# Adding the experts' rows straight into the output, by halves, and gathering expert 1's rows one stage later

## The chip, the cores and the metric

One core of one Trainium2 chip runs the whole layer as one program. The metric is the device time of an execution in microseconds (us). TensorE is PE in the profile, VectorE DVE, ScalarE ACT, GpSimd POOL, and SyncE SP, which here only issues DMAs.

## The reference: two attentions and a mixture of experts

x is [2, 2048, 256] in float32, so 4096 tokens of 256 numbers. The part that the change touches is the last one:

```python
xn = _layernorm(x, axis=-1)
x = x + _L0_attn_ref(xn, ...) + _L0_ffn_ref(xn, ...)

# in _L0_ffn_ref: attention with biases, then
hidden = resid + (ctx @ o_w + o_b)
xt = layer_norm(hidden, ln2_w, ln2_b).reshape(T, D)
probs = softmax(xt @ router_w)            # T = 4096 tokens, E = 16 experts
m1, m2 = one-hot of each token's first and second expert
loc1 = cumsum(m1) - 1; loc2 = cumsum(m2) - 1 + m1.sum(0)
C = 2 * ceil(T / E)                       # 512 slots an expert
m1 = m1 * (loc1 < C); m2 = m2 * (loc2 < C)
g1, g2 = gates of the kept choices, divided by their sum
xin = rows of xt by expert and slot       # [16, 512, 256]
h = gelu(xin @ fc1_w + fc1_b)             # F = 1024
eout = (h @ fc2_w + fc2_b) * (1.0 - 0.2)
moe_out = for each token, the sum of gate * eout over its kept slots
return resid + moe_out
```

A choice beyond an expert's 512 slots is dropped, and slots that no token takes stay empty. With the reference's own inputs the choices are very uneven. The slots taken are 14, 4, 0, 0, 4, 0, 0, 512, 512, 0, 0, 0, 0, 512, 0, 0 for experts 0 to 15: 1558 of 8192.

## The kernel before, in words

Six stages follow one another, each a block of five instruction streams (one for each engine) that ends in a barrier of all five. Within a stage the order on each engine is written out by hand and the streams meet by semaphores.

- stage_a normalises x and makes the queries, keys and values of both attentions in DRAM; stage_b does both attentions, 16 groups of four heads; stage_c (block from L741) adds projection, residual and second norm, writes the tokens' rows xt to the DRAM tensor xt_scratch, keeps `base` (everything that a token gets beside the experts) in SBUF and computes the router's logits.
- stage_d, the routing stage (block from L975). PE and ACT add the first attention's projection to `base`, and SP stores it, eight pieces of 512 KB, as the first 4096 rows of the DRAM tensor sum_scratch (L1081). DVE finds each token's two experts and slots and turns them round: for each of the 64 groups of 128 slots, `rows_of` holds the token's row to read, `sums_of` the row to add to, `slot_gates` the gate. An empty slot reads row 0 and has a row of its own beyond 4095 to add to; sum_scratch has 512 such spare rows. As soon as `rows_of` is there, POOL issues gather_rows (L729) for experts 0 and 1, four indirect DMAs each, 128 rows of 1 KB in one, into the two buffers of `xin`.
- stage_e, the expert stage (block from L1233). For each of 16 experts PE multiplies the rows (turned, L1404) with fc1 (L1417, eight blocks of 128 features) and the result with fc2 (L1432, four tiles of 128 slots). Every matrix is split in a high and a low part, so each product is three matmuls. The transpositions of expert e+1 stand between the two products of expert e. ACT applies gelu (L1385, L1386), DVE makes the low parts (L1328, L1351, L1336) and takes fc2's result out as `eout`, in two halves of two tiles (L1361), which needs b2, fc2's bias for all experts, scaled once by POOL (L1292). POOL then, for each expert: four gathers for expert e+2 (once PE has turned expert e's rows), four scalings of eout by the slots' gates (L1300), and four indirect DMAs that add the 128 rows of each to sum_scratch in DRAM (L1306, the scatter-adds). Two experts' rows can name the same token, so expert e's scatter-adds wait for those of e-1 to land (`summed`). SP loads the weights of the next expert as soon as DVE has split those of the present one.
- stage_f (block from L1449): SP copies the first 4096 rows of sum_scratch to the output, eight DMAs of 512 KB, DRAM to DRAM, and waits for them.

POOL waits once for both halves of an expert's eout before its scalings:

```python
pool.wait_ge(added, e * 2 + 4)
```

Of the kernel before, what the change touches and what calls it, by code (L numbers as in the profile page):

```python
# [16 lines left out]
ALU = mybir.AluOpType  # L17
ACT = mybir.ActivationFunctionType
AX = mybir.AxisListType
F32 = mybir.dt.float32  # L20
# [5 lines left out]
P = 128  # L26
B, S, D = 2, 2048, 256
T = B * S
# [3 lines left out]
CAP = 2 * (T // E)  # L32
# [16 lines left out]
KEEP = 1.0 - 0.2  # L49
SPARE = CAP  # L50
CELLS = E * CAP // P
# [912 lines left out]
def stage_d(nc, weights, scratch, const, keep, late):  # L964


    fc1_w, fc2_w = weights
    ctx_dram, xt_dram, sum_dram = scratch
    base, logits, numbers = keep
# [5 lines left out]
    with ExitStack() as ctx:  # L975
# [88 lines left out]
        @block.sync  # L1064
        def _(sp):
            def load(c):
                b, cc = c // (NCH // B), c % (NCH // B)
                groups = ctx_dram[(B + b) * HG:(B + b + 1) * HG, :, cc * CH:(cc + 1) * CH]
                sp.dma_start(attT[:, c % PLACES], groups.rearrange("(k g) r t -> (g r) k t", k=KD)).then_inc(att_in[c % PLACES], 16)

            tiles = sum_dram[0:T, :].rearrange("(t p) d -> p t d", p=P)
            for c in range(PLACES):
                load(c)
            sp.dma_start(w1[:, :, :], fc1_w[0].rearrange("(h p) f -> p h f", p=P)).then_inc(w1_in, 16)
            sp.dma_start(w2[:, :, :], fc2_w[0].rearrange("(f p) d -> p f d", p=P)).then_inc(w2_in, 16)
            for c in range(NCH):
                sp.wait_ge(base_ready, 2 * (c + 1))
                if c + PLACES < NCH:
                    load(c + PLACES)
                cut = slice(c * TPC, (c + 1) * TPC)  # L1080
                sp.dma_start(tiles[:, cut], base[:, cut, :]).then_inc(base_stored, 16)  # L1081
            sp.wait_ge(base_stored, 16 * NCH)
# [16 lines left out]
        def _(pool):  # L1099
# [5 lines left out]
            pool.wait_ge(rows_ready, 1)  # L1105
            for e in range(2):
                gather_rows(pool, e, xt_dram, xin, rows_of, rows_in)

# [108 lines left out]
def stage_e(nc, weights, scratch, const, keep):  # L1217
# [6 lines left out]
    fc1_w, fc2_w, fc2_b = weights  # L1224
    xt_dram, sum_dram = scratch
    (w1, w2, w1_parts, xin, rows_of, sums_of, slot_gates), (w1_in, w2_in, w1_high, w1_split, rows_in) = keep
# [6 lines left out]
    with ExitStack() as ctx:  # L1233
# [55 lines left out]
        @block.gpsimd  # L1289
        def _(pool):  # L1290
            pool.wait_ge(b2_in, 16)
            pool.tensor_scalar(b2[:, :, :], b2[:, :, :], KEEP, None, ALU.mult).then_inc(b2_scaled, 1)  # L1292
            for e in range(E):
                i, u = e // 2, e % 2
                if e + 2 < E:
                    pool.wait_ge(turned, KD * (e + 1))
                    gather_rows(pool, e + 2, xt_dram, xin, rows_of, rows_in)
                pool.wait_ge(added, e * 2 + 4)
                for j in range(CAP // P):
                    pool.tensor_scalar(scaled[:, u, j, :], eout[:, u, j, :], slot_gates[:, TPE * e + j:TPE * e + j + 1], None,  # L1300
                                       ALU.mult).then_inc(weighed, 1)
                pool.wait_ge(weighed, (e + 3) * (CAP // P))
                if e > 0:
                    pool.wait_ge(summed[1 - u], TURN * (i + u))  # L1304
                for j in range(CAP // P):
                    pool.indirect_dma_start(out=sum_dram, out_offset=bass.IndirectOffsetOnAxis(ap=sums_of[:, TPE * e + j:TPE * e + j + 1], axis=0),  # L1306
                                            in_=scaled[:, u, j, :], in_offset=None, compute_op=ALU.add).then_inc(summed[u], 16)
            for u in range(2):
                pool.wait_ge(summed[u], TURN * (E // 2))
# [135 lines left out]

def stage_f(nc, out, sum_dram):

    PIECES = 8
    with ExitStack() as ctx:  # L1449
        stored = ctx.enter_context(nc.semaphore("f_stored"))  # L1450
        block = ctx.enter_context(nc.Block())
        dst = out.rearrange("b s d -> (b s d)").rearrange("(n p w) -> n p w", n=PIECES, p=P)
        src = sum_dram[0:T, :].rearrange("t d -> (t d)").rearrange("(n p w) -> n p w", n=PIECES, p=P)

        @block.sync
        def _(sp):
            for n in range(PIECES):
                sp.dma_start(dst[n], src[n]).then_inc(stored, 16)
            sp.wait_ge(stored, 16 * PIECES)


def load_constants(nc, w, const, b1_rows):
# [81 lines left out]
def layer(nc, x, w, out):  # L1544
# [6 lines left out]
    xt_dram = nc.dram_tensor("xt_scratch", [T, D], F32).ap()  # L1551
    sum_dram = nc.dram_tensor("sum_scratch", [T + SPARE, D], F32).ap()
    with ExitStack() as ctx:
# [18 lines left out]
        with ExitStack() as late:  # L1572
# [11 lines left out]
            with nc.sbuf_tensor("base", [P, NTILE, D], F32) as base, nc.sbuf_tensor("logits", [P, NTILE, E], F32) as logits, \  # L1584
                    nc.sbuf_tensor("numbers", [P, NUMBERS_SIZE], F32) as numbers:
                stage_c(nc, x, (xn_dram, ctx_dram, xt_dram, rec_dram), const, ((base, logits, numbers), last))
                stage_d(nc, (w["fc1_w"], w["fc2_w"]), (ctx_dram, xt_dram, sum_dram), const, (base, logits, numbers), keep)
            stage_e(nc, (w["fc1_w"], w["fc2_w"], w["fc2_b"]), (xt_dram, sum_dram), const, keep)
        stage_f(nc, out, sum_dram)


# [23 lines left out]
```

## Time and profile before

| | us |
|---|---|
| median of 3 runs | 2424.3 (2418.44 to 2435.3) |
| the profiled execution | 2424.48 |
| its span, first to last instruction | 2422.8 |
| mean granted TensorE clock | 0.947 of full speed |

By stage, from the timeline: the routing stage runs from 1913.2 to 2007.8 us, the expert stage to 2405.7, the copy to the end. Times of the trace count from the span's start. Busy time of an indirect DMA on POOL is the time in which POOL writes its descriptors; the rows move later.

### The profile page before, as it was taken

The numbers are of one execution on the slowest core, as the hardware profiler recorded it, in microseconds if no ns is written. First come the engines' busy times: TensorE is split into PE (matmuls) and PEld (weight loads), VectorE is DVE, ScalarE is ACT, GpSimd is POOL, SyncE is SP. The second block draws the span as 40 slices with busy tenths as digits, with TensorE's granted clock in tenths as the row PEclk, the third lists the DMA queues.
The fourth block names the chain that finished last, engine by engine and source line by source line (L and its number), as shares of the span: only waits on it lengthen the run. The fifth ranks groups of instructions, "written<-read, shape, count | busy, mean of one in ns | idle before, by whom it ended". The sixth has DMA issues, their size and how long they took to land. (4 is left out here: it accounts for less than half of the span.)

```text
span 2422.8 us, 45249 instructions
## 1 busy us (share of the span) xinstructions
PE 2236.6 (92%) x15977; PEld 1286.5 (53%) x15977; DVE 1901.1 (78%) x5771; ACT 1514.4 (63%) x3190; POOL 507.1 (21%) x405
## 2 busy tenths in 40 slices
PE   5995999999999999999999999999996778999994
PEld 2553444444444444444444444444435667999993
DVE  3553999989899899899899899989917886666661
ACT  2541378778788787787787778878871113545441
POOL 0001000110210201101101001001005115778773
PEclk9997699999999899999899999989997798999997
DMA  5997325345154253451632534516018435666563
GB/s 153 294 264 220 36 28 64 43 57 63 20 73 55 37 64 41 59 63 23 78 44 39 71 38 56 63 21 81 3 19 237 155 86 136 145 137 128 133 130 87
DMA packets 145315, 214.54 MB, mean 89 GB/s; under 512 B 54560, under 2 KB 108000, under 8 KB 136672
## 3 DMA queue, kind: packets, MB, share of 16 engines
q1 hardware_dynamic: 132832, 195.27, 40.8%
q0 software_dynamic: 12288, 16.79, 5.6%
q8 instruction: 108, 1.77, 0.3%
q14 instruction: 87, 0.71, 0.1%
HBM read 138.43 MB, written 76.02 MB: 89 GB/s over the span
## 5 line engine op out<-in xcount | busy, mean ns | idle before, releaser
L653 ACT ACTIVATE probs<-s_banks 128x512 f32<-128x512 f32 (+3 forms) x2560 | 1183.5, 539 | 321.9 <-PE s_banks L604 193.1
L690 DVE TENSOR_REDUCE rowmax<-m_banks 128x1 f32<-128x512 f32 x1536 | 966.5, 683 | 64.8 <-PE m_banks L615 59.2
L615 PE MATMUL m_banks<-ks,qs 48*128 48x512 f32 (+3 forms) x2560 | 827.6, 436 | 28.8 <-PEq L89 20.5
L604 PE MATMUL s_banks<-qs,ks 50*128 50x512 f32 (+3 forms) x2560 | 820.3, 429 | 14.7 <-ACT probs L653 7.7
L633 PE MATMUL v_bank<-probs,vs 128*32 128x512 f32 (+3 forms) x5120 | 616.7, 554 | 0.0
L604 PEld LDWEIGHTS s_banks<-qs,ks 50*128 50x128 f32 x2560 | 402.7, 188 | 394.9 <-ACT probs L653 358.5
L615 PEld LDWEIGHTS m_banks<-ks,qs 48*128 48x128 f32 x2560 | 415.9, 193 | 262.0 <-DVE rowmax L690 163.2
L687 DVE CUSTOM_DVE_ANT_0 unused<-m_banks,c_maskq 128x128 bf16<-128x128 f32 (+3 forms) x1024 | 466.8, 486 | 58.5 <-issue 51.2
L550 POOL CAST nparts<-negmax 128x16 fp32r<-128x16 f32 x64 | 12.6, 196 | 1185.5 <-DVE negmax L696 1185.5
L1432 PE MATMUL e_banks<-w_parts,hid_parts 128*128 128x256 f32 x1536 | 189.7, 284 | 1.4 <-DVE hid_parts L1351 1.4
L576 PE MATMUL s_banks<-c_identb,c_later_col 64*128 64x64 bf16 x1024 | 189.2, 197 | 0.0
L576 PE MATMUL s_banks<-c_identb,c_later_col_swapped 64*128 64x64 bf16 x1024 | 189.0, 197 | 0.0
L1432 PEld LDWEIGHTS e_banks<-w_parts,hid_parts 128*128 128x128 f32 x1536 | 185.7, 192 | 2.9 <-DVE hid_parts L1351 2.5
L633 PEld LDWEIGHTS v_bank<-probs,vs 128*32 128x32 f32 x5120 | 101.3, 108 | 156.4 <-issue 81.0
L1417 PE MATMUL e_banks<-xinT,w_parts 128*128 128x512 f32 x768 | 178.8, 392 | 1.5 <-DVE xinT L1336 1.5
L1417 PEld LDWEIGHTS e_banks<-xinT,w_parts 128*128 128x128 f32 x768 | 144.3, 189 | 31.3 <-issue 1.9
L1385 ACT ACTIVATE hid_parts<-e_banks,c_b1T 128x512 fp32r<-128x512 f32 x128 | 89.5, 700 | 113.6 <-PE e_banks L1417 102.8
L1351 DVE TENSOR_TENSOR hid_parts<-e_hid,hid_parts 128x512 fp32r<-128x512 f32 x128 | 100.0, 794 | 46.2 <-ACT e_hid L1386 45.9
L1300 POOL TENSOR_SCALAR scaled<-eout,slot_gates 128x256 f32<-128x256 f32 x64 | 99.4, 1564 | 63.9 <-DVE eout L1361 63.9
L1306 POOL DMA_INDIRECT sum_scratch<-scaled,sums_of x64 | 106.6, 1666 | 19.1 <-issue 14.6
L576 PEld LDWEIGHTS s_banks<-c_identb,c_later_col 64*128 64x128 bf16 x1024 | 95.8, 96 | 26.4 <-issue 5.4
L576 PEld LDWEIGHTS s_banks<-c_identb,c_later_col_swapped 64*128 64x128 bf16 x1024 | 95.3, 96 | 24.2 <-issue 13.3
(185 smaller groups left out, 1740.9 us busy)
## 6 DMA issues: line engine op xcount, KB each, us to landing
w<-in_L_ffn_fc_w SPq DMA_DIRECT2D x32, 1024.0 KB, 5.3
qs<-q_scratch SPq DMA_DIRECT2D x96, 256.0 KB, 8.3
ks<-k_scratch SPq DMA_DIRECT2D x96, 256.0 KB, 10.0
q_scratch<-parts SPq DMA_DIRECT2D x64, 256.0 KB, 4.5
k_scratch<-parts SPq DMA_DIRECT2D x64, 256.0 KB, 4.7
v_scratch<-vt SPq DMA_DIRECT2D x16, 512.0 KB, 7.9
v_in<-v_scratch SPq DMA_DIRECT2D x32, 256.0 KB, 10.7
qs<-mrows SPq DMA_DIRECT2D x512, 2.0 KB
```

Source lines behind the costliest of these rows:

```text
L576: ins = pe.matmul(bank[:, j * HALF:(j + 1) * HALF], const[mask][rows, :], const["identb"][rows, rows], start=False, stop=j == 1)
L604: ins = pe.matmul(bank, ks[rows, slot, h // 2, k * P:(k + 1) * P], qs[rows, slot, h // 2, q * CH + first:(q + 1) * CH], start=True, stop=n ...
L615: pe.matmul(room(("M", NM * group + n))[:, 0:width], qs[rows, slot, h // 2, t * P:(t + 1) * P], ks[rows, slot, h // 2, c * CH:c * CH + wid ...
L633: ins = pe.matmul(v_bank[rows, first:CH], vs[:, slot, k, rows], probs[:, (n * GH + h) % PR, 0:CH - first], start=k == 0, stop=k == TPC * ( ...
L653: act.activation(probs[:, n % PR, 0:width], s_banks[:, (NS * group + n) % SRING, 0:width], ACT.Exp, scale=SCALE).then_inc(p_ready, 1)
L687: dve.tensor_tensor_reduce(unused[:, h, 0:width], scores, const["maskq"][:, CH - width:CH], 1.0, NEG, ALU.add, ALU.max, out).then_inc(m_us ...
L690: dve.tensor_reduce(out, scores, AX.X, ALU.max).then_inc(m_used, 1)
L1300: pool.tensor_scalar(scaled[:, u, j, :], eout[:, u, j, :], slot_gates[:, TPE * e + j:TPE * e + j + 1], None, ALU.mult).then_inc(weighed, 1)
L1306: pool.indirect_dma_start(out=sum_dram, out_offset=bass.IndirectOffsetOnAxis(ap=sums_of[:, TPE * e + j:TPE * e + j + 1], axis=0), in_=scal ...
L1351: dve.tensor_tensor(hid_parts[:, LO, f, :], hid[:, f % HRING, :], f32(hid_parts[:, HI, f, :]), ALU.subtract).then_inc(hid_split, 1)
L1417: last = pe.matmul(banks[:, HBANK + f % HRING, :], w1_parts[:, a, h, f * P:(f + 1) * P], xinT[:, b, h, :], start=h == 0 and (a, b) == PASS ...
L1432: last = pe.matmul(banks[:, OBANK + n, j * D:(j + 1) * D], hid_parts[:, a, f, tile * P:(tile + 1) * P], w2_parts[:, b, f, :], start=f == 0 ...
```

## The change

The stages add to the output `out` instead of sum_scratch, from stage_d's stores on; sum_scratch, its spare rows and stage_f are gone. The scatter-adds get a bounds check: an index above 4095 is to be skipped. stage_d gathers only expert 0's rows, and expert 1's are the first thing that POOL issues in stage_e. And POOL takes eout by halves: two scalings and two scatter-adds when the first half is there, two and two for the second; the wait for expert e-1's scatter-adds stands ahead of the first half's.

```diff
-SPARE = CAP
...
-            tiles = sum_dram[0:T, :].rearrange("(t p) d -> p t d", p=P)
+            tiles = out.rearrange("b s d -> (b s) d").rearrange("(t p) d -> p t d", p=P)
...
             pool.wait_ge(rows_ready, 1)
-            for e in range(2):
-                gather_rows(pool, e, xt_dram, xin, rows_of, rows_in)
+            gather_rows(pool, 0, xt_dram, xin, rows_of, rows_in)
...
         @block.gpsimd
         def _(pool):
+            gather_rows(pool, 1, xt_dram, xin, rows_of, rows_in)
             pool.wait_ge(b2_in, 16)
...
-                pool.wait_ge(added, e * 2 + 4)
-                for j in range(CAP // P):
-                    pool.tensor_scalar(scaled[:, u, j, :], eout[:, u, j, :], slot_gates[:, TPE * e + j:TPE * e + j + 1], None,
-                                       ALU.mult).then_inc(weighed, 1)
-                pool.wait_ge(weighed, (e + 3) * (CAP // P))
-                if e > 0:
-                    pool.wait_ge(summed[1 - u], TURN * (i + u))
-                for j in range(CAP // P):
-                    pool.indirect_dma_start(out=sum_dram, out_offset=bass.IndirectOffsetOnAxis(ap=sums_of[:, TPE * e + j:TPE * e + j + 1], axis=0),
-                                            in_=scaled[:, u, j, :], in_offset=None, compute_op=ALU.add).then_inc(summed[u], 16)
+                for half in range(2):
+                    pool.wait_ge(added, e * 2 + 2 + half + 1)
+                    pair = range(half * TPE // 2, (half + 1) * TPE // 2)
+                    for j in pair:
+                        pool.tensor_scalar(scaled[:, u, j, :], eout[:, u, j, :], slot_gates[:, TPE * e + j:TPE * e + j + 1], None,
+                                           ALU.mult).then_inc(weighed, 1)
+                    pool.wait_ge(weighed, (e + 2) * TPE + pair[-1] + 1)
+                    if e > 0 and half == 0:
+                        pool.wait_ge(summed[1 - u], TURN * (i + u))
+                    for j in pair:
+                        pool.indirect_dma_start(out=rows,
+                                                out_offset=bass.IndirectOffsetOnAxis(ap=sums_of[:, TPE * e + j:TPE * e + j + 1], axis=0),
+                                                in_=scaled[:, u, j, :], in_offset=None, bounds_check=T - 1, oob_is_err=False,
+                                                compute_op=ALU.add).then_inc(summed[u], 16)
...
-def stage_f(nc, out, sum_dram):
...
-            for n in range(PIECES):
-                sp.dma_start(dst[n], src[n]).then_inc(stored, 16)
-            sp.wait_ge(stored, 16 * PIECES)
...
-    sum_dram = nc.dram_tensor("sum_scratch", [T + SPARE, D], F32).ap()
...
-        stage_f(nc, out, sum_dram)
```

On POOL, from the end of the routing stage into expert 0 (the branches L975 and L1289 are the stage's end and the next one's start). Before:

```order
L729 DMA xin<-xt_scratch,rows_of 128x256 [waits rows_ready]
L729 DMA xin<-xt_scratch,rows_of 128x256 x7
L975 UNCONDITIONAL_BRANCH
L1289 UNCONDITIONAL_BRANCH [waits barrier_Pool_Activation_PE_DVE_SP_gather]
L1292 TENSOR_SCALAR b<-b 128x4096 [waits b2_in]
L729 DMA xin<-xt_scratch,rows_of 128x256 [waits e_turned]
L729 DMA xin<-xt_scratch,rows_of 128x256 x3
L1300 TENSOR_SCALAR scaled<-eout,slot_gates 128x256 [waits e_added]
L1300 TENSOR_SCALAR scaled<-eout,slot_gates 128x256 x3
L1306 DMA sum_scratch<-scaled,sums_of 4608x256 [waits weighed]
L1306 DMA sum_scratch<-scaled,sums_of 4608x256 x3
```

The same place with the change:

```order
L728 DMA xin<-xt_scratch,rows_of 128x256 [waits rows_ready]
L728 DMA xin<-xt_scratch,rows_of 128x256 x3
L974 UNCONDITIONAL_BRANCH
L1288 UNCONDITIONAL_BRANCH [waits barrier_Pool_Activation_PE_DVE_SP_gather]
L728 DMA xin<-xt_scratch,rows_of 128x256 x4
L1292 TENSOR_SCALAR b<-b 128x4096 [waits b2_in]
L728 DMA xin<-xt_scratch,rows_of 128x256 [waits e_turned]
L728 DMA xin<-xt_scratch,rows_of 128x256 x3
L1302 TENSOR_SCALAR scaled<-eout,slot_gates 128x256 [waits e_added]
L1302 TENSOR_SCALAR scaled<-eout,slot_gates 128x256
L1308 DMA out<-scaled,sums_of 4096x256 [waits weighed]
L1308 DMA out<-scaled,sums_of 4096x256
```

Four gathers have moved behind the stage's boundary and ahead of the scaling of b2 (the tile b), and the first pair of scalings is followed at once by its pair of scatter-adds. The last expert on POOL, before and with the change:

```order
L1300 TENSOR_SCALAR scaled<-eout,slot_gates 128x256 [waits e_added]
L1300 TENSOR_SCALAR scaled<-eout,slot_gates 128x256 x3
L1306 DMA sum_scratch<-scaled,sums_of 4608x256 [waits summed0,weighed]
L1306 DMA sum_scratch<-scaled,sums_of 4608x256 x3
L1233 UNCONDITIONAL_BRANCH [waits summed1,summed0]
```

```order
L1302 TENSOR_SCALAR scaled<-eout,slot_gates 128x256 [waits e_added]
L1302 TENSOR_SCALAR scaled<-eout,slot_gates 128x256
L1308 DMA out<-scaled,sums_of 4096x256 [waits summed0,weighed]
L1308 DMA out<-scaled,sums_of 4096x256
L1302 TENSOR_SCALAR scaled<-eout,slot_gates 128x256 [waits e_added]
L1302 TENSOR_SCALAR scaled<-eout,slot_gates 128x256
L1308 DMA out<-scaled,sums_of 4096x256 [waits weighed]
L1308 DMA out<-scaled,sums_of 4096x256
L1232 UNCONDITIONAL_BRANCH [waits summed1,summed0]
```

The instructions are the same but for their order; the last two scatter-adds stand behind the second half's two scalings alone.

## Rows read from the trace of the kernel before

**Rows 1.** The page: busy time of the engines; the chain that ended last.

```profile
PE 2236.6 (92%) x15977; PEld 1286.5 (53%) x15977; DVE 1901.1 (78%) x5771; ACT 1514.4 (63%) x3190; POOL 507.1 (21%) x405
...
POOL 11%; issue 4%; PE 1%; DVE 0%; ACT 0%; POOLq 0%; ACTq 0%; DVEq 0%
```

**Rows 2.** Windows: columns, then busy us (instructions) of twelve experts in a row.

```profile
core 0: us, PE busy (x) PEld busy (x) DVE busy (x) ACT busy (x) POOL busy (x), PEclk, DMA share, GB/s
2063.14:2342.50 279.36, 279.36 (x1825) 256.06 (x1824) 187.04 (x240) 136.93 (x222) 215.37 (x144) 1.00 0.63 135
```

**Rows 3.** Timeline of POOL in expert 12 (start us, us, ...); a DVE group.

```profile
2320.06 6.59 POOL L1300 TENSOR_SCALAR scaled<-eout,slot_gates 128x256 f32<-128x256 f32 x4 [2.93 <-DVE eout L1361]
...
2335.99 1.90 POOL L729 DMA_INDIRECT xin<-xt_scratch,rows_of  x1 [0.30 <-issue]
...
L1351 DVE TENSOR_TENSOR hid_parts<-e_hid,hid_parts 128x512 fp32r<-128x512 f32 x96 | 70.3, 742 | 34.1 <-ACT e_hid L1386 33.9
```

**Rows 4.** Timeline: end of the routing stage, start of the expert stage.

```profile
1991.45 1.20 POOL L729 DMA_INDIRECT xin<-xt_scratch,rows_of  x1 [38.05 <-DVE rows_of L1208]
...
2000.49 0.95 POOL L729 DMA_INDIRECT xin<-xt_scratch,rows_of  x1 [0.30 <-issue]
...
2007.87 1.94 PE L1404 MATMUL e_banks<-c_ident,xin 128*128 128x128 f32 x8 [17.21 <-PEq L975]
...
2008.16 0.35 SPq L1277 DMA_DIRECT2D b<-in_L_ffn_fc_b  x1
```

**Rows 5.** Timeline and a window: the last expert and the final copy.

```profile
2388.27 0.69 DVE L1361 SCALAR_TENSOR_TENSOR eout<-e_banks,b 128x512 f32<-128x512 f32 x1 [4.96 <-PE e_banks L1432]
2389.07 3.62 POOL L1300 TENSOR_SCALAR scaled<-eout,slot_gates 128x256 f32<-128x256 f32 x4 [7.89 <-DVE eout L1361]
2392.97 1.59 POOL L1306 DMA_INDIRECT sum_scratch<-scaled,sums_of  x1 [0.28 <-POOL scaled L1300]
...
2398.58 1.55 POOL L1306 DMA_INDIRECT sum_scratch<-scaled,sums_of  x1 [0.31 <-issue]
2405.76 5.46 SPq L1458 DMA_DIRECT2D out<-sum_scratch  x8
...
2402.00:2405.70 3.70, 0.00 (x0) 0.00 (x0) 0.00 (x0) 0.00 (x0) 0.00 (x0) 0.50 0.00 0
```

**Rows 6.** Timeline: the boundary before the routing stage.

```profile
1913.23 1.28 ACT L1087 ACT_TABLE_LOAD   x1 [0.27 <-PEq L741]
```

**Rows 7.** Windows behind the gathers; the last column is GB/s.

```profile
1992.50:2006.60 14.10, 0.00 (x0) 0.00 (x0) 0.16 (x1) 0.00 (x0) 6.80 (x8) 0.55 0.70 74
...
2006.50:2007.00 0.50, 0.00 (x0) 0.00 (x0) 0.00 (x0) 0.00 (x0) 0.00 (x0) 0.50 0.01 0
```

**Rows 8.** Timeline and a window: head of the expert stage.

```profile
2011.30 12.69 PE L1417 MATMUL e_banks<-xinT,w_parts 128*128 128x512 f32 x48 [1.49 <-DVE xinT L1336]
...
2015.31 10.59 POOL L1292 TENSOR_SCALAR b<-b 128x4096 f32<-128x4096 f32 x1 [13.87 <-DMA b<-in_L_ffn_fc_b]
...
2016.92 10.20 DVE L1351 TENSOR_TENSOR hid_parts<-e_hid,hid_parts 128x512 fp32r<-128x512 f32 x5 [2.29 <-ACT e_hid L1386]
...
2023.83 1.03 PE L1404 MATMUL e_banks<-c_ident,xin 128*128 128x128 f32 x8
...
2034.94 0.68 DVE L1361 SCALAR_TENSOR_TENSOR eout<-e_banks,b 128x512 f32<-128x512 f32 x1
...
2039.51 11.07 PE L1417 MATMUL e_banks<-xinT,w_parts 128*128 128x512 f32 x48
...
2009.00:2011.00 2.00, 0.81 (x4) 0.41 (x2) 1.22 (x2) 1.19 (x2) 0.00 (x0) 0.50 0.93 385
```

**Rows 9.** Line L1306: ns lowest, median, highest; the software queue: packets, MB, share.

```profile
L1306 POOL DMA_INDIRECT sum_scratch<-scaled,sums_of x64: 1547/1637/2052, 2047.4 to 2398.6; - x64
...
q0 software_dynamic: 12288, 16.79, 5.6%
```

**Rows 10.** Waits of the DMA queue: us in total, times, longest.

```profile
SPq L1449 <- DMA out<-sum_scratch: 11.2, 1, 11.2
```

More of the change, by code:

```diff
@@ L967, in stage_d @@
     fc1_w, fc2_w = weights
-    ctx_dram, xt_dram, sum_dram = scratch
+    ctx_dram, xt_dram, out = scratch
     base, logits, numbers = keep
@@ L1224, in stage_e @@
     fc1_w, fc2_w, fc2_b = weights
-    xt_dram, sum_dram = scratch
+    xt_dram, out = scratch
+    rows = out.rearrange("b s d -> (b s) d")
     (w1, w2, w1_parts, xin, rows_of, sums_of, slot_gates), (w1_in, w2_in, w1_high, w1_split, rows_in) = keep
@@ L1443, in _ @@
             expert(E // 2 - 1, 1, False)
-def stage_f(nc, out, sum_dram):
[L1448 to L1456, printed above, removed]
-            for n in range(PIECES):
-                sp.dma_start(dst[n], src[n]).then_inc(stored, 16)
-            sp.wait_ge(stored, 16 * PIECES)
 def load_constants(nc, w, const, b1_rows):
@@ L1586, in layer @@
                 stage_c(nc, x, (xn_dram, ctx_dram, xt_dram, rec_dram), const, ((base, logits, numbers), last))
-                stage_d(nc, (w["fc1_w"], w["fc2_w"]), (ctx_dram, xt_dram, sum_dram), const, (base, logits, numbers), keep)
-            stage_e(nc, (w["fc1_w"], w["fc2_w"], w["fc2_b"]), (xt_dram, sum_dram), const, keep)
-        stage_f(nc, out, sum_dram)
+                stage_d(nc, (w["fc1_w"], w["fc2_w"]), (ctx_dram, xt_dram, out), const, (base, logits, numbers), keep)
+            stage_e(nc, (w["fc1_w"], w["fc2_w"], w["fc2_b"]), (xt_dram, out), const, keep)
 _ATTN = ["W_dq", "W_uq", "W_dkv", "W_uk", "W_uv", "W_o"]
```

## The prediction, made before the changed kernel was run

> **What bounds the kernel now.** I read the page first, then the windows of the last stages, then the timelines of the three places that the change touches. Over the whole span PE is busy 92% and POOL 21% [rows 1], and yet the chain that ended last gives POOL the largest share of what it names, 11% [rows 1]. That is a warning about how such a chain is read: through the expert loop it steps from POOL instruction to POOL instruction, but in twelve successive experts PE is busy 279.36 us of 279.36 us [rows 2], 23.28 us each, at the full granted clock (1.00, the 2.4 GHz level), and POOL waits about 2.9 us for DVE's eout before each batch of scalings [rows 3]. So the loop is PE's. What isn't PE's lies at its two ends. Between the last gather of the routing stage and the first transposition of the expert stage no engine computes for 6.4 us [rows 4]. And from the last eout half to the end of the span 33.8 us pass (2388.96 to 2422.8) with PE idle [rows 5], of which the final copy takes 17. The change works on both ends.
>
> **The four gathers of expert 1 leave the routing stage.** POOL issues eight gathers there, one every 1.29 us (starts 1991.45 to 2000.49, seven steps), and has written the last one's descriptors at 2001.44; PE, DVE and SP resume at 2007.87 to 2008.16 [rows 4]. A stage's end alone does not cost that: at the boundary before, where no indirect DMA runs, ACT begins the routing stage's first instruction after 0.27 us of idle time [rows 6]. What fills the 6.4 us is data: the DMA engines carry the gathered rows at 74 GB/s until about 2006.5 [rows 7], some 13.5 us for eight gathers, 1.7 us each, slower than they are issued. So the stage ends 1.4 us behind the last gathered row. With four gathers the data should end 4 x 1.7 = 6.7 us earlier (1999.8), and the issuing, over at 1996.3, stays under it. The other end of the bound is that the boundary follows the issuing: 4 x 1.26 = 5.0 us. I take **-6.7**, since the 6.4 us of silence between issue and resumption are explained by the data and by nothing else that I see.
>
> **They come back at the head of the expert stage.** There POOL waited 13.9 us for the bias b2, which landed 7.1 us after its issue [rows 8], so four gathers of 1.3 to 1.6 us fit ahead of the scaling of b2; expert 1's rows are read by PE at 2023.83, 16 us after the stage's start, and issue (6 us) plus 4 x 1.7 us of data is under that. The price is traffic: 0.5 MB of rows beside b2 and two weight loads. In the profile b2's scaling on POOL (10.6 us) stretches five DVE subtractions to 10.20 us, where five take 3.7 us in the loop (mean 742 ns), and the first expert lasts 28.2 us (2011.30 to 2039.51) in place of 23.3 [rows 2, 3, 8]. If b2 lands later, that stretch moves later by as much. 0.5 MB more at the 385 GB/s of that window is 1.4 us [rows 8]. Bounds: -1 (the stretch falls where DVE is needed less) to +4.9 (the loss that this expert already shows, once more). I take **+1**. Behind the scaling come expert 2's gathers, not read until 2050; expert 0's eout needs the scaled b2 only at 2034.94, 9 us after it is there, so that cover holds a delay up to 9 us. The gathers also move from a stretch where DVE is idle (0.95 us each) to one where it works, where the same instruction took up to 1.90 us [rows 3, 4]; 4 x 1 us more would still be under b2's landing plus its 9 us.
>
> **Scaling and adding by halves.** In the loop POOL's work is 4 scalings (6.6 us, mean 1.6 beside DVE), 4 scatter-adds of 1.64 and 4 gathers, 0.3 us apart [rows 3, 9]; the halves neither add nor remove an instruction there, they start two scalings and two scatter-adds 5.65 us sooner, at the first eout half. Nothing on PE waits for that, so in the loop it is worth **0**: PE covers it. Queued behind POOL's new wait for the second half are the gathers for expert e+2. From the first eout POOL needs 1.8 + 0.3 + 3.5 us for the first half, from 5.7 on 3.3 + 0.3 + 3.5 + 0.3 for the second (to 13.1) and 5.9 for the gathers (to 19.0); the next eout comes at 23.3. POOL's slack is so 4.3 us an expert. At the last expert it counts. Eout's halves are ready at 2383.31 (DVE's idle time before the second starts there) and 2388.96 [rows 5]. Before: four scalings of 0.91 us, then four scatter-adds to 2400.13. After: the first half is done by 2389.0, hidden under PE's second half; behind 2388.96 stand two scalings (1.8), 0.3, and two scatter-adds (1.59 + 0.31 + 1.55), which ends at 2394.6. That is **-5.5**.
>
> **No final copy.** The copy's first DMA is issued at 2405.76; the span ends at 2422.8, with the last wait for its landing lasting 11.2 us to 2422.4 [rows 5, 10]. All of it goes: **-17.0**. What is late next is the landing of the last scatter-add: from the end of its issue to the copy's start 5.6 us pass (1.9 us of data until 2402.0, then 3.7 us of silence) [rows 5]. I keep these 5.6 us as the kernel's new end; the former end had 0.4 us after its last landing, which the 5.6 already hold as a stage's end.
>
> **The bounds check.** No row shows an indirect DMA with one. I bound its price by the nearest row, the scatter-add itself [rows 9]: from -1.6 us each (the indices of empty slots write no descriptors) to a doubling, +1.6 us; I take no change, as all 64 scatter-adds lie between 1.55 and 2.05 us [rows 9], whatever their indices. In the loop either is covered. What it drops is real: by the reference on its own inputs only 1558 of the 8192 expert slots hold a token, and experts 14 and 15 hold none, so the last scatter-adds should move nothing. Then the 1.9 us of data behind the last issue go in part: bounds 0 to -1.9, I take **-1**.
>
> **Sum.** -6.7 + 1 - 5.5 - 17.0 - 1 = -29.2 us. The profiled execution took 2424.5 us (span 2422.8), 0.2 above the median of the runs, 2424.3. Forecast 2395.2 us, 1.2% faster. Storing the routing stage's base rows into out in place of a scratch costs nothing that I can name: same eight stores of 512 KB.
>
> **Rivals.**
> (a) The boundary does not follow the gathers' data: ending a stage that holds indirect DMAs has a fixed price. For it: the 3.7 us of silence at the other boundary, which no data fills. Against it: 0.3 us at the plain one, and data up to 1.4 us before the stage resumes. Then 2395.2 + 6.7 = 2402. Chance 0.12.
> (b) The first expert gives it back: the four gathers, beside DVE's work at 1.90 us each, and their traffic push b2's scaling into the last DVE work that PE waits for. Then that expert's loss of 4.9 us comes once more in place of my 1: 2399.1. Against it: the 9 us of cover. Chance 0.08. The Trainium skill (SBUF — State Buffer, SBUF: two separate sides) speaks for it: a DMA issued from GpSimd can't write its descriptors while VectorE runs a two-port operation, about 620 ns becoming about 3100 ns; by that, an estimate, the gathers would take 12.4 us. The trace agrees in kind, 0.95 against 1.90 us, not in size.
> (c) The bounds check makes each scatter-add dearer, by less than POOL's slack. Up to 1.07 us each (4.3 / 4) the loop hides it; the tail shows all four of the last expert, +4.3: 2399.5. For it: a comparison per index. Chance 0.10.
> (d) Slower: the bounds-checked scatter-add takes so long that POOL becomes the loop's bound. It decides from 1.07 us more; each expert then lasts 4x - 4.3 us longer. The 29 us are eaten at x = 1.53 (16 x 1.8 us), slower by 1% it is from x = 1.9, more than twice today's duration; at x = 2.5 it is 2395 + 16 x 5.7 = 2486. Nothing in the profile speaks for such a price, and nothing excludes it. Chance 0.03.
> (e) The check skips nothing: the transfers still run for all rows. Then only my -1 is missing: 2396. Chance 0.12.
> (f) With nothing to move, the last scatter-adds complete as fast as the gathers did, 1.4 us behind [rows 4, 7], in place of my 4.6: 2392. For it: the silence of 3.7 us stood behind accumulating writes, of which none is left at the end. Against it: the same silence may be the queue's own. Chance 0.12. The Trainium skill (DMA: Bandwidth & Descriptors, Anatomy of one DMA — SWDGE (gpsimd) path) says that most of a DMA's fixed cost of about 2.0 us is the wait for the write's receipt, longest from HBM; by that, an estimate, the tail would be 2 us and the time 2392.6. The trace agrees so far that 1.4 us stand behind writes to SBUF and 3.7 behind writes to HBM.
> The forecast itself: 0.43.
>
> **How the numbers follow.** About 1% (24 us, a time under 2400.1) is what a measurement of this kernel tells from no change; its three runs lie from 2418.4 to 2435.3. The forecast, (b), (c), (e) and (f), 0.85 together, end 0.5 to 8 us under 2400, which the scatter of medians eats about one time in five; (a) ends above. Faster by over 1%: 0.66; within 1%: 0.31; slower: 0.03. Range 2388 to 2404: below, no price at the expert stage's head (-2), rival (f) (-3.2) and a little more for scatter-adds that write fewer descriptors; above, rival (a) with 2 us of (b) on top. It leaves out (d) and (a) with all of (b).
>
> **What would show each step.** Routing stage: first transposition 10 us after the first gather's issue, not 16.4, with four gathers between. Expert stage: b2's scaling starts 8 to 9 us after the stage's start; the first expert lasts 28 to 30 us. Loop: PE busy throughout, 23.3 us an expert, POOL waiting about 4 us for the first eout half and, in the gap between halves, none after. Tail: last scatter-add's issue ends 5.7 us behind the last eout half, the span ends 4 to 6 us later, and no copy. The software queue's bytes fall from 16.79 MB [rows 9] to about 10 MB if empty slots are skipped. Wrong it would be if scatter-adds take over 2.7 us, if PE idles between experts, or if PE's first transposition waits as long as before.

## The result, and the profile after

| | before | with the change |
|---|---|---|
| median of the comparison's runs (4 each) | 2429.51 | 2399.11 |
| lowest, highest | 2418.44, 2435.3 | 2397.43, 2401.85 |
| the profiled execution, its span | 2424.48, 2422.8 | 2401.85, 2400.1 |

The ratio is 0.9871, with a 95% interval of 0.9835 to 0.9907: 1.3% faster. The forecast was 2395.2 (2388 to 2404) against 2424.3, and 1.2%.

In the two profiles the routing stage's first matmul, L1032 and L1033, stands at 1917.5 us before and at 1922.7 us after, behind stages that the change does not touch. From it to the span's end are 505.3 us before and 477.4 us after: **-27.9**. This stretch is compared below, since the attention ahead of it moves by more than a term of the sum from run to run (1917.5 to 1936.5 in ten of the eleven profiles).

The page of the changed kernel, with the software queue's packets, MB and share, and the chain:

```profile
span 2400.1 us, 45293 instructions
...
PE 2243.1 (93%) x15977; PEld 1289.1 (54%) x15977; DVE 1901.0 (79%) x5771; ACT 1513.8 (63%) x3190; POOL 495.8 (21%) x405
...
q0 software_dynamic: 12288, 10.05, 3.3%
...
POOL 11%; issue 5%; DVE 0%; PE 0%; ACT 0%; POOLq 0%; DVEq 0%; ACTq 0%
```

The chain still gives POOL its largest share, 11% [rows 1]. The queue moves 10.05 MB where it moved 16.79 [rows 9]: 6.74 MB less, and 6634 empty slots of 1 KB are 6.79 MB. So the check skips. But the packets are 12288 as before, for 16384 rows gathered and added: skipping takes bytes and no packets.

The timeline of the boundary, and two windows behind the gathers (last column GB/s); these answer to [rows 4, 7]:

```profile
1996.86 1.20 POOL L728 DMA_INDIRECT xin<-xt_scratch,rows_of  x1 [37.32 <-DVE rows_of L1206]
...
2000.89 0.94 POOL L728 DMA_INDIRECT xin<-xt_scratch,rows_of  x1 [0.30 <-issue]
2005.85 1.94 PE L1408 MATMUL e_banks<-c_ident,xin 128*128 128x128 f32 x8 [9.79 <-PEq L974]
...
2006.14 0.35 SPq L1276 DMA_DIRECT2D b<-in_L_ffn_fc_b  x1
2006.45 0.94 POOL L728 DMA_INDIRECT xin<-xt_scratch,rows_of  x1 [4.61 <-POOLq L974]
...
2009.29 13.26 PE L1421 MATMUL e_banks<-xinT,w_parts 128*128 128x512 f32 x48 [1.49 <-DVE xinT L1340]
```

```profile
2004.50:2005.00 0.50, 0.00 (x0) 0.00 (x0) 0.00 (x0) 0.00 (x0) 0.00 (x0) 0.50 0.23 33
2005.00:2005.50 0.50, 0.00 (x0) 0.00 (x0) 0.00 (x0) 0.00 (x0) 0.00 (x0) 0.50 0.00 0
```

From the first gather's issue to PE's first transposition 8.99 us pass, in place of 16.42: **-7.4**. Data ends between 2004.5 and 2005, about 1 us ahead of PE, as it ended 1.4 us ahead before. The silence behind the last issue is 4.0 us (2001.83 to 2005.85) in place of 6.4, so it is no fixed amount. POOL's next gather comes 0.6 us after PE, at the other side of the boundary.

The head of the expert stage; this answers to [rows 8]:

```profile
2014.69 10.59 POOL L1292 TENSOR_SCALAR b<-b 128x4096 f32<-128x4096 f32 x1 [3.47 <-DMA b<-in_L_ffn_fc_b]
...
2014.91 11.59 DVE L1355 TENSOR_TENSOR hid_parts<-e_hid,hid_parts 128x512 fp32r<-128x512 f32 x5 [2.25 <-ACT e_hid L1390]
...
2022.38 1.03 PE L1408 MATMUL e_banks<-c_ident,xin 128*128 128x128 f32 x8
...
2038.88 11.07 PE L1421 MATMUL e_banks<-xinT,w_parts 128*128 128x512 f32 x48
```

b2 landed 8.55 us after its issue (2006.14 to 2014.69), not 7.1, and the first expert lasts 29.6 us (2009.29 to 2038.88), not 28.2: **+1.4**. The five subtractions beside POOL's scaling take 11.59 us, not 10.20. That group hides what happens. The line's row (lowest, median and highest ns) shows that it is a single long one:

```profile
L1355 DVE TENSOR_TENSOR hid_parts<-e_hid,hid_parts x128: 675/692/9187, 2014.9 to 2377.4; 128x512 fp32r<-128x512 f32 x128
```

The first subtraction of the group is held for 9.19 us, beside the scaling; the four behind it make up the other 2.4. Before, the one that is held takes 7.80 us, 1.4 less: the whole difference of the first expert.

The loop, in one window over 15 experts (columns as in [rows 2]), and POOL in expert 13 (it answers to [rows 3]):

```profile
2034.00:2382.00 348.00, 348.00 (x2270) 318.88 (x2269) 226.82 (x296) 169.56 (x274) 247.25 (x172) 1.00 0.45 109
```

```profile
2337.19 1.83 POOL L1302 TENSOR_SCALAR scaled<-eout,slot_gates 128x256 f32<-128x256 f32 x2 [2.93 <-DVE eout L1365]
2339.85 1.65 POOL L1308 DMA_INDIRECT out<-scaled,sums_of  x1 [0.83 <-POOL scaled L1302]
...
2342.85 4.38 POOL L1302 TENSOR_SCALAR scaled<-eout,slot_gates 128x256 f32<-128x256 f32 x2
```

PE is busy throughout, 348.00 us of 348.00: **0**. POOL waits 2.93 us for the first eout half in most experts, and 1.20 us in a few. Two things are new: 0.78 to 0.83 us pass between scalings and scatter-adds where 0.28 passed [rows 5], and this twice an expert; and the second pair of scalings begins 0.2 us behind its eout half (2342.63), without a wait, while the last descriptors of the first pair are still being written (to 2343.46).

The tail, which answers to [rows 5]:

```profile
2385.71 1.60 POOL L1308 DMA_INDIRECT out<-scaled,sums_of  x1 [1.09 <-issue]
2387.61 1.57 POOL L1308 DMA_INDIRECT out<-scaled,sums_of  x1 [0.30 <-issue]
2387.66 0.69 DVE L1365 SCALAR_TENSOR_TENSOR eout<-e_banks,b 128x512 f32<-128x512 f32 x1 [4.97 <-PE e_banks L1436]
2388.64 2.40 POOL L1302 TENSOR_SCALAR scaled<-eout,slot_gates 128x256 f32<-128x256 f32 x2
2391.82 1.60 POOL L1308 DMA_INDIRECT out<-scaled,sums_of  x1 [0.78 <-POOL scaled L1302]
2393.72 1.57 POOL L1308 DMA_INDIRECT out<-scaled,sums_of  x1 [0.30 <-issue]
```

The 1.09 us ahead of the last expert's first scatter-add are 0.3 more than elsewhere; e6, e7 and e8 show 0.78 there. From the second eout half (2388.35) to the end of the last issue (2395.29) are 6.9 us, before 11.2: **-4.2**. From there to the span's end are 4.8 us, before 22.7: **-17.9**. In sum -7.4 + 1.4 - 4.2 - 17.9 = -28.1, against the 27.9 of the whole stretch.

### The profile page after: what moved, and what is told of

Same layout as the page of the kernel before. It is cut to its first block and busy times, and to the rows that moved or that the text cites. A ratio compares the mean times of both kernels' runs of the same rounds, so it can differ in the third digit from the quotient of the medians.

```text
span 2400.1 us, 45293 instructions
## 1 busy us (share of the span) xinstructions
PE 2243.1 (93%) x15977; PEld 1289.1 (54%) x15977; DVE 1901.0 (79%) x5771; ACT 1513.8 (63%) x3190; POOL 495.8 (21%) x405
## 3 DMA queue, kind: packets, MB, share of 16 engines
q0 software_dynamic: 12288, 10.05, 3.3%
## 5 line engine op out<-in xcount | busy, mean ns | idle before, releaser
L614 PE MATMUL m_banks<-ks,qs 48*128 48x512 f32 (+3 forms) x2560 | 827.5, 436 | 28.6 <-PEq L88 20.5
L1308 POOL DMA_INDIRECT out<-scaled,sums_of x64 | 113.1, 1767 | 36.9 <-POOL scaled L1302 23.3
```

What stands on the lines that cost most here:

```text
L614: pe.matmul(room(("M", NM * group + n))[:, 0:width], qs[rows, slot, h // 2, t * P:(t + 1) * P], ks[rows, slot, h // 2, c * CH:c * CH + wid ...
L1308: pool.indirect_dma_start(out=rows, out_offset=bass.IndirectOffsetOnAxis(ap=sums_of[:, TPE * e + j:TPE * e + j + 1], axis=0), in_=scaled[: ...
```

## The experiments

Each part of the change alone, and the check taken away, came first. All are read at their places, and by the stretch from the routing stage's first matmul to the end (505.3 before, 477.4 changed); the medians of single parts hardly stand out of the runs' scatter. The places of every profile, in us: from the first gather's issue to PE's first transposition, with the number of gathers between; from b2's issue to the start of its scaling; the longest subtraction; the first expert; the stretch.

| | boundary (gathers) | b2 | subtraction | first expert | stretch |
|---|---|---|---|---|---|
| before | 16.42 (8) | 7.15 | 7.80 | 28.2 | 505.3 |
| changed | 8.99 (4) | 8.55 | 9.19 | 29.6 | 477.4 |
| e1 | 8.98 (4) | 9.71 | 9.20 | 29.6 | 498.9 |
| e2 | 16.09 (8) | 8.82 | 8.78 | 30.9 | 501.3 |
| e3 | 16.08 (8) | 7.81 | 8.46 | 28.9 | 488.5 |
| e4 | 9.30 (4) | 9.91 | 9.40 | 29.8 | 477.3 |
| e6 | 6.79 (4, skipping) | 7.50 | 8.14 | 28.6 | 476.0 |
| e7 | 9.28 (4) | none | 0.69 | 25.2 | 473.3 |
| e8 | 6.82 (4, skipping) | none | 0.69 | 25.0 | 472.5 |
| e9 | 9.29 (4) | 8.97 | 8.78 | 30.8 | 543.8 |
| e10 | 9.35 (4) | 9.72 | 9.21 | 29.7 | 475.9 |

The same gathers give boundaries of 8.98 to 9.35 us and of 16.08 to 16.42, so a place carries some 0.3 us either way. And wherever POOL scales b2 the first expert is 20.4 to 20.5 us plus the longest subtraction, in seven profiles; e2, at a lower clock, and e9, with more work on POOL, are over a microsecond longer.

### e1_gather_only

```diff
-            for e in range(2):
-                gather_rows(pool, e, xt_dram, xin, rows_of, rows_in)
+            gather_rows(pool, 0, xt_dram, xin, rows_of, rows_in)
...
+            gather_rows(pool, 1, xt_dram, xin, rows_of, rows_in)
             pool.wait_ge(b2_in, 16)
```

> The kernel before, with expert 1's four gathers moved to the head of the expert stage and nothing else. My theory (the stage's end waits for the gathered rows to land): from the first gather's issue to PE's first transposition 8.9 us in place of 16.4, as in the changed kernel; the first expert 1.4 us longer; together about -6, so near 2418 against 2424. Rival, a fixed price at the end of a stage with indirect DMAs: 16.4 minus the issue of four, 11.4 us, time -3.6. Rival, given back at the head of the expert stage: first expert over 33 us and no gain.

```profile
1992.96 1.20 POOL L729 DMA_INDIRECT xin<-xt_scratch,rows_of  x1 [38.03 <-DVE rows_of L1207]
...
2001.94 1.94 PE L1404 MATMUL e_banks<-c_ident,xin 128*128 128x128 f32 x8 [9.77 <-PEq L975]
...
2005.38 12.83 PE L1417 MATMUL e_banks<-xinT,w_parts 128*128 128x512 f32 x48 [1.49 <-DVE xinT L1336]
...
2035.02 10.16 PE L1417 MATMUL e_banks<-xinT,w_parts 128*128 128x512 f32 x44
```

The timeline shows 8.98 us from first gather to transposition, and a first expert of 29.6 us: both as in the changed kernel, so the two terms belong to this part alone. Median 2420.8, ratio 0.9973 (0.9943 to 1.0003), stretch 498.9, -6.4 us. The fixed price is refuted, and the full give-back.

### e2_halves_only

The loop over halves of the change, with `out=sum_dram` and no `bounds_check`, in the kernel before.

> The kernel before, with the scalings and scatter-adds by halves, still into the scratch, without the bounds check and with the final copy. My theory: nothing in the loop (23.3 us an expert), and from the second eout half of the last expert to the end of the last scatter-add's issue 5.7 us in place of 11.2: -5.5. With 0.28 us between scalings and scatter-adds if the check makes the 0.78 us seen in the changed kernel; with 0.78 and about 6.2 to 6.7 us if the order by halves makes it.

```profile
2427.75 0.69 DVE L1365 SCALAR_TENSOR_TENSOR eout<-e_banks,b 128x512 f32<-128x512 f32 x1 [4.97 <-PE e_banks L1436]
...
2430.64 1.60 POOL L1308 DMA_INDIRECT sum_scratch<-scaled,sums_of  x1 [0.28 <-POOL scaled L1302]
2432.54 1.57 POOL L1308 DMA_INDIRECT sum_scratch<-scaled,sums_of  x1 [0.30 <-issue]
```

Its profiled execution ran at a lower granted clock (0.929 in the mean, 0.947 before), so its stretch is not compared, and only the places with PE idle are read: 5.67 us from the second eout half (2428.44) to the end of the issue, the -5.5 of the forecast to the tenth, and 0.28 us ahead of the scatter-adds. Median 2429.31, ratio 0.9977 (0.9948 to 1.0006). That the halves are worth nothing in the loop is read from the changed kernel and e4, where PE is busy throughout.

### e3_no_copy_only

The changed kernel with the gathers as in the kernel before, and

```diff
-                for half in range(2):
-                    pool.wait_ge(added, e * 2 + 2 + half + 1)
...
+                pool.wait_ge(added, e * 2 + 4)
+                for j in range(CAP // P):
...
+                    pool.indirect_dma_start(out=rows, ..., bounds_check=T - 1, oob_is_err=False, compute_op=ALU.add)
```

> The changed kernel with eight gathers in the routing stage and all four scalings ahead of all four scatter-adds, so only the straight adding with its bounds check is left of the change. My theory: the copy's 17.0 us go and about 1 us behind the last issue, -17 to -18, near 2406. If the copy's time were partly needed anyway (the landing of accumulating writes in the output being slower than in a scratch), -14 or less. Wait ahead of the first scatter-add of an expert 0.78 us if the bounds check makes it, 0.28 if not.

```profile
2393.58 0.69 DVE L1361 SCALAR_TENSOR_TENSOR eout<-e_banks,b 128x512 f32<-128x512 f32 x1 [4.96 <-PE e_banks L1432]
...
2398.78 1.59 POOL L1306 DMA_INDIRECT out<-scaled,sums_of  x1 [0.78 <-POOL scaled L1300]
...
2404.39 1.55 POOL L1306 DMA_INDIRECT out<-scaled,sums_of  x1 [0.30 <-issue]
```

From second eout half to the end 16.3 us (2394.27 to 2410.6), before 33.8: -17.5, of which the issue's end takes back 0.5 (11.67 for 11.17) by the wait of 0.78 us. Stretch 488.5, -16.8; the other 0.7 is a first expert 0.65 us longer than before, without any gathers there. Median 2413.87, ratio 0.9925 (0.989 to 0.9959). The three parts, e2's by its place, add: -6.4 - 5.5 - 16.8 = -28.7 against -27.9. The tail accounts for 0.8: the waits ahead of scatter-adds cost 0.5 us in e3 and 1.3 in the changed kernel, where halves and check meet.

### e4_unchecked

The changed kernel with `out=sum_dram` and its 512 spare rows, without `bounds_check`, and without the final copy.

> The changed kernel adding into a scratch with spare rows and without the bounds check; nothing is copied to the output, which so stays unwritten. My theory: the loop the same; the wait ahead of scatter-adds 0.28 us in place of 0.78; the software queue moves 16.8 MB again in place of 10.05; behind the last issue 5.6 us in place of 4.8, so within 1 us of the changed kernel's time in sum. Rival, the check is what costs: 3 us or more faster than the changed kernel. Rival, the skipping is what helps: 3 us or more slower.

```profile
2400.11 0.69 DVE L1365 SCALAR_TENSOR_TENSOR eout<-e_banks,b 128x512 f32<-128x512 f32 x1 [4.97 <-PE e_banks L1436]
...
2402.99 1.60 POOL L1308 DMA_INDIRECT sum_scratch<-scaled,sums_of  x1 [0.28 <-POOL scaled L1302]
2404.90 1.57 POOL L1308 DMA_INDIRECT sum_scratch<-scaled,sums_of  x1 [0.30 <-issue]
```

0.28 us again, 16.79 MB again, 5.67 us to the issue's end and 5.7 us behind it (span 2412.2). Against the changed kernel: -1.3 and +0.9. Stretch 477.3 against 477.4, median 2404.86, ratio 0.9869 (0.9815 to 0.9923) against 0.9871: what the check costs POOL and what skipping saves in the tail nearly cancel. The edit changes the tensor added to as well as the check, so the 0.5 us could belong to either by this run; e6, whose first gather gets the check, keeps its tensor and starts 0.7 us later behind its indices, speaks for the check. It is worth having only because it lets the rows go straight into the output.

### e6_skip_gathers, e7_b2_early, e8_both

What is left at the boundary and in the first expert, taken apart. e6:

```diff
+            pool.memset(xin[:, :, :, :], 0.0).then_inc(xin_clear, 1)
+            pool.wait_ge(xin_clear, 1)
             pool.wait_ge(rows_ready, 1)
-            gather_rows(pool, 0, xt_dram, xin, rows_of, rows_in)
+            gather_rows(pool, 0, xt_dram, xin, sums_of, rows_in)
...
-                                in_offset=bass.IndirectOffsetOnAxis(ap=rows_of[...], axis=0))
+                                in_offset=bass.IndirectOffsetOnAxis(ap=rows_of[...], axis=0),
+                                bounds_check=T - 1, oob_is_err=False)
```

> The changed kernel whose gathers too read by the indices with spare values and skip what is out of bounds, so that empty slots move nothing (expert 0's four gathers move 14 rows, expert 1's 4); xin is cleared once while POOL is idle. The indices are ready 0.9 us later. Theory (the boundary follows the gathered data): from the first gather's issue to PE's first transposition 6.5 to 8 us in place of 8.99, since only the issue of 5 us and a completion are left. Rival, it follows the issue and a fixed price: 8.99 as before. At the expert stage's head b2 lands in 7.1 us again in place of 8.55 and the first expert lasts 28.2 to 28.8 us in place of 29.6 if the gathers' traffic made the difference. In all -1 to -2 us against the changed kernel, which a median hardly tells; the places tell.

```profile
2012.84 1.26 POOL L728 DMA_INDIRECT xin<-xt_scratch,sums_of  x1 [38.77 <-DVE sums_of L1212]
...
2017.04 1.00 POOL L728 DMA_INDIRECT xin<-xt_scratch,sums_of  x1 [0.30 <-issue]
2019.63 1.94 PE L1409 MATMUL e_banks<-c_ident,xin 128*128 128x128 f32 x8 [9.03 <-PEq L975]
...
2023.06 12.80 PE L1422 MATMUL e_banks<-xinT,w_parts 128*128 128x512 f32 x48 [1.49 <-DVE xinT L1341]
...
2051.61 8.58 PE L1422 MATMUL e_banks<-xinT,w_parts 128*128 128x512 f32 x37
...
q0 software_dynamic: 12288, 3.28, 1.0%
```

6.79 us in place of 8.99, 1.6 us behind the end of the fourth issue (2018.04), with 3.28 MB in the queue: without data the boundary goes back towards the issue. That is what tells "waits for data" from a fixed price. The first expert lasts 28.55 us, a microsecond less than with the gathers' bytes. But the gathers start 76.3 us behind the routing stage's first matmul, not 74.2 (1922.7 to 1996.86): the indices with spare values come later and POOL starts 1.0 us behind them (2011.85 to 2012.84) in place of 0.3, together 2.1 us where 0.9 was expected, and what the boundary gives that takes. What is left is the first expert's microsecond and 0.3 in the tail: stretch 476.0, -1.4. Median 2407.66, ratio 0.9893 (0.9843 to 0.9942), which can't show it.

e7:

```diff
# routing stage, SP and ACT
+            sp.dma_start(b2[:, :, :], fc2_b.rearrange("(a e) d -> a e d", a=1).to_broadcast([P, E, D])).then_inc(b2_in, 16)
...
+            act.wait_ge(b2_in, 16)
+            act.activation(b2[:, :, :], b2[:, :, :], ACT.Copy, scale=KEEP)
# expert stage, POOL
-            pool.wait_ge(b2_in, 16)
-            pool.tensor_scalar(b2[:, :, :], b2[:, :, :], KEEP, None, ALU.mult).then_inc(b2_scaled, 1)
```

> The changed kernel with b2 loaded in the routing stage and scaled there by ACT, which has nothing left to do; POOL has no scaling at the head of the expert stage. Theory (POOL's scaling of b2 stretches DVE's subtractions, and that is the first expert's loss): five subtractions take 3.5 to 4 us in place of 11.6, and the first expert lasts 25 to 26 us in place of 29.6, the rest of its excess over 23.3 being the clock's lower level at its start; -4 against the changed kernel, near 2395. Rival, the loss is the clock and the weight loads: still 28 us or more, no gain. The routing stage unchanged.

```profile
2007.26 13.01 PE L1418 MATMUL e_banks<-xinT,w_parts 128*128 128x512 f32 x48 [1.49 <-DVE xinT L1338]
...
2012.89 0.69 DVE L1353 TENSOR_TENSOR hid_parts<-e_hid,hid_parts 128x512 fp32r<-128x512 f32 x1 [2.23 <-ACT e_hid L1387]
...
2032.50 11.07 PE L1418 MATMUL e_banks<-xinT,w_parts 128*128 128x512 f32 x48
```

The subtractions are 0.69 us each again, none is held, and the first expert lasts 25.2 us, 4.4 less. The edit takes b2's load from the head as well as its scaling; it is the held subtraction that says which of the two cost the time. The 1.9 us left over 23.3 go with the clock: it is granted at 0.50 (the 1.2 GHz level) until 2011, and the expert's first 48 products take 13.01 us in place of 11.07. Stretch 473.3. Median 2393.5, ratio 0.9843 (0.9798 to 0.9888).

e8 is both edits together.

> The changed kernel with both: gathers that skip empty slots, and b2 scaled by ACT in the routing stage. If the two places are independent the gains add, -5 to -6 against the changed kernel, ratio to the kernel before about 0.985. Rival: the clock's rise comes later in the first expert and takes part of it back, -3.

Boundary 6.82 us, first expert 25.0, stretch 472.5, 4.9 us under the changed kernel: -2.2 at the boundary, -4.6 in the first expert and -0.3 in the tail, less the 2.1 us by which the gathers start later. The gains of the places add, but not those of the edits (-1.4 and -4.1): the microsecond that e6 won in the first expert was of the loss that e7 removes. On top of e7, e6's edit is worth 0.8 us of the stretch, little more than a place carries by chance. Median 2395.38, ratio 0.9853 (0.9807 to 0.9898). By their places e7 and e8 beat the changed kernel by 4 to 5 us; their intervals overlap its own, and the medians alone would not say so.

### e9_busy_pool

```diff
+                for n in range(4):
+                    pool.memset(filler[:, :], 0.0).then_inc(filled, 1)
+                    pool.wait_ge(filled, 4 * e + n + 1)
                 if e + 2 < E:
```

> The changed kernel with four idle fills of 1.8 us on POOL in each expert, 7.2 us more of POOL's work, nothing else. My theory (POOL has about 3 us of slack an expert, 2.9 measured as its wait for the first eout half): POOL becomes the loop's bound, 27.5 to 27.7 us an expert in place of 23.3, 60 to 68 us longer in all. Rival, POOL's lateness is absorbed by the two buffers: under 25 us an expert.

The timeline of POOL and a window of 300 us in the loop:

```profile
2204.79 8.88 POOL L1298 MEMSET filler<- 128x2048 f32 x4
...
2219.37 1.84 POOL L1307 TENSOR_SCALAR scaled<-eout,slot_gates 128x256 f32<-128x256 f32 x2
...
2247.89 1.85 POOL L1307 TENSOR_SCALAR scaled<-eout,slot_gates 128x256 f32<-128x256 f32 x2
...
2100.00:2400.00 300.00, 262.16 (x1601) 237.82 (x1600) 185.31 (x218) 126.20 (x203) 259.51 (x172) 0.94 0.38 96
```

28.5 us from expert to expert (2219.37 to 2247.89), PE busy 262 us of 300, and POOL no longer waits for eout. The fills came to 8.9 us, not 7.2, and 20.4 (23.3 less the wait of 2.9) + 8.9 less some overlap is the period; the loop took up 3.7 us of them. So rival (d)'s mechanism is real: POOL can become the bound. Its single execution took 2478.9 us, 77 us over the 2401.85 of the changed kernel's profiled one, more than the 60 to 68 expected with the shorter fills.

### e10_plain_last

```diff
-                                                compute_op=ALU.add).then_inc(summed[u], 16)
+                                                **({"compute_op": ALU.add} if e < E - 1 else {})).then_inc(summed[u], 16)
```

> The changed kernel whose last four scatter-adds (expert 15, whose slots are all empty, so that the check skips all rows) are plain scatters without the addition. What is open: 4.8 us pass from the end of the last one's issue to the end of the program, with no byte moved, where the other boundary needs 1.8 us with next to none (skipping gathers). If completing an accumulating DMA costs the difference: 4.8 becomes 2 to 3 us. If it is the waiting on the DMAs' semaphores by POOL ahead of the stage's end, or the program's end: 4.8 stays. The program 2400 either way.

```profile
2391.66 0.69 DVE L1365 SCALAR_TENSOR_TENSOR eout<-e_banks,b 128x512 f32<-128x512 f32 x1 [4.96 <-PE e_banks L1436]
...
2395.07 1.03 POOL L1308 DMA_INDIRECT out<-scaled,sums_of  x1 [0.80 <-POOL scaled L1302]
2396.40 0.98 POOL L1308 DMA_INDIRECT out<-scaled,sums_of  x1 [0.30 <-issue]
```

Behind the last issue (2397.38) 4.7 us pass to the span's end (2402.1): as with the addition. So it is not the accumulating that takes them. What does, the waiting on the semaphores or the end itself, stays open. A plain scatter's issue took 1.0 us, an accumulating one's 1.6, both with every row skipped. Its one execution took 2403.86 us.

## Why the prediction was right, step by step

- **Gathers out of the routing stage**: -6.7 forecast, -7.4 measured, alone and together (8.98 and 8.99 us); over all profiles the difference is 6.7 to 7.4. The reason, the boundary follows the gathered data, is shown by e6, where data was taken away and the boundary came 2.2 us sooner. Rival (a) is out. Its price was wrong as well: a fixed price behind the issue would still have given the 5.0 us of issuing that the forecast itself names as its other bound, so 2396.9 us and not 2402.
- **Gathers at the head of the expert stage**: +1 forecast, +1.4 measured, by the mechanism named: b2 lands later, POOL's scaling moves with it, and the subtraction that it holds ends later by as much. That b2 came 1.45 us later here, where 1.4 was forecast, is luck: its landing takes 7.15, 7.81 and 8.82 us (e2) with no gathers there, 7.50 with gathers that move next to nothing and 8.55 to 9.91 with them; and where it is latest (e1, e4, e10) the first expert hardly grows further (29.6 to 29.8), since the held subtraction doesn't (9.20 to 9.40). The forecast read five subtractions stretched to 2 us each; it is one that is held. e7 shows that this scaling makes 4.4 us of the first expert's excess over 23.3 us. Rival (b) did not come: the gathers beside DVE took 0.94 to 1.02 us there, not the 3.1 us that the Trainium skill (SBUF — State Buffer, SBUF: two separate sides) gives for locked-out descriptor writing. The longest at this head in any run was 1.97 us, in e7.
- **Halves**: 0 in the loop, as measured. In the tail -5.5 forecast, -4.2 measured; e2 alone gives the 5.5. The mis-sized term is the check's: the forecast took its issue price as nothing. The issue itself is unchanged, 1.57 to 1.60 us, but 0.5 us stands ahead of each pair, so the first half is through at 2389.18, 0.8 us behind the second eout half instead of level with it, and the second pair pays 0.5 again: 1.3 us. Of these 1.0 is the check's; 0.3 is the longer wait of 1.09 us, whose cause no run shows (without it, in e6 and e7, the issue ends 6.6 us behind the second eout half). Rival (c) came in kind, a check that costs, though not for each index.
- **The loop's slack**: forecast 4.3 us, measured 2.93, and 1.20 in a few experts. The forecast had nothing for the check's 0.5 us twice; in e4, without the check, POOL waits 4.25 and 2.94 us by turns. Covered by PE, so free, but the room for dearer scatter-adds was smaller than rivals (c) and (d) reckoned.
- **The copy and the landing**: -18 forecast (-17.0 and -1), -17.9 measured. The tail of 4.6 us was 4.8. Rival (f), 1.4 us, and the estimate of 2 us from the Trainium skill's fixed cost of a DMA (DMA: Bandwidth & Descriptors, Anatomy of one DMA — SWDGE (gpsimd) path) do not hold: with nothing written 4.8 us stay, without the addition 4.7. Rival (e) is out by the bytes.
- **Sum**: -29.2 forecast, -27.9 over the stretch. The time itself, 2395.2 against 2399.1, misses by 1.3 us of this and by where the untouched attention ended, which moves from execution to execution: 5.2 us later in the profiled one (2401.85) than in that of before. The comparison's other median moved too, from 2424.3 to 2429.51, so that the medians differ by 30.4 us; that this is near 29.2 rests in part on luck, the 27.9 of the stretch do not.

## What to carry to other kernels

Ask at each stage's end which transfers are still in flight, not only which instructions are left: a stage that issued indirect DMAs closed when their rows had landed, and moving four of them over the boundary gave more than their issue. Read a change of few microseconds at its places in the profile and by a stretch that begins behind the noisy part; of the three parts run alone, the medians show only the copy's clear of no change. Don't take a group's mean for its members: five subtractions in 11.6 us were one of 9.2 us and four as usual. And a long one-off instruction on an idle engine isn't always free: b2's scaling on POOL held one subtraction of DVE and cost 4.4 us until ACT did it.

## What the runs showed of the hardware

- Skipped rows of a bounds-checked indirect DMA move no bytes, and the packets stay: 12288 with 16.79, 10.05 and 3.28 MB. The issue stays as long (median 1.66 us, 1.64 before, 1.65 in e4), so skipping spares data, not POOL.
- With the check 0.5 us more pass ahead of a group of scatter-adds, not in them: 0.78 to 0.83 us against 0.28, the same for a group of four (e3) and of two. Ahead of e6's first checked gather it was 0.7 us more, ahead of the gathers behind b2's scaling nothing (0.17 us, 0.18 unchecked).
- An accumulating scatter's descriptors took 1.6 us to write, a plain one's 1.0 (e10).
- One POOL instruction of 10.6 us (128x4096 float32) held one DVE subtraction for 7.8 to 9.4 us; the subtractions behind it took 0.7 us. With the work on ACT none was held.
- The end of the kernel behind scatters took 4.7 to 4.8 us from the last issue with no data in flight, the end of the routing stage behind skipping gathers 1.6 us. Why they differ is open.
